# Normalisation of the second stage on ScalarE, and a re-ordered seam between two stages of a transformer block

## The reference, cut to what matters

```python
x = X                                           # 16 sequences of 512 tokens, 256 wide, fp32
x = x + attn_a(layernorm(x))                    # 16 heads of 64, softmax, exact gelu; attn_a adds its own input
x = x + ffn(layernorm(x))                       # weights quantised to -1, 0, 1; 256 -> 1024 -> relu -> 256
x = x + attn_b(layernorm(x))                    # 16 heads of 16, rotary embedding, softmax, biases
x = x + ffn(layernorm(x))                       # the same ffn again
# layernorm(x) = (x - mean) / sqrt(var + 1e-5), per token; quantise(W) = clip(round(W / (mean|W| + 1e-5)), -1, 1)
```

## Time and profile before

| | us |
|---|---|
| three runs | 3824.11, 3825.49, 3829.05 (median 3825.49) |
| the profiled execution, device time | 3828.33 |
| its span, first to last instruction | 3826.2 |
| PE busy in the span | 3658.7 (96%) |
| DVE, ACT, POOL busy | 2724.2 (71%), 2318.7 (61%), 1927.7 (50%) |
| seam, roughly | 2150 to 2300 |

### The profile page before, as it was taken

The page is one execution under the profiler, slowest core; times in us unless marked ns, Lnnn a source line. Parts: engine busy times, 40 slices in busy tenths (PEclk is TensorE's granted clock), DMA queues, the critical chain, the costliest instruction groups (busy, mean ns, idle before and its releaser), DMA issues.

```text
span 3826.2 us, 64594 instructions
## 1 busy us (share of the span) xinstructions
PE 3658.7 (96%) x23938; PEld 2458.9 (64%) x23938; DVE 2724.2 (71%) x4335; ACT 2318.7 (61%) x4501; POOL 1927.7 (50%) x1218
## 2 busy tenths in 40 slices
PE   8999999999999999999999868999999999999987
PEld 5777777777777777777777554555555555555534
DVE  6766667667666666766667757888888888887772
ACT  5666656565565656656665435666666666666654
POOL 4555555555555555555555443455555555554412
PEclk9999999999999999999999988999999999999998
DMA  2000000000000000000000022333333333333220
GB/s 78 7 12 1 12 12 12 1 12 12 1 12 12 12 1 12 12 1 12 12 4 12 24 47 51 53 58 58 58 58 62 57 59 59 56 57 57 51 46 17
DMA packets 90933, 114.15 MB, mean 30 GB/s; under 512 B 10752, under 2 KB 64384, under 8 KB 90624
## 3 DMA queue, kind: packets, MB, share of 16 engines
q1 hardware_dynamic: 90624, 110.02, 14.3%
HBM read 33.43 MB, written 25.17 MB: 15 GB/s over the span
## 4 chain that ended last, share of the span: by engine, by line
PE 82%; DVE 8%; POOL 4%; ACT 3%; issue 2%; SPq 0%; DMA 0%; DVEq 0%; POOLq 0%; ACTq 0%
PE ps_o L616 12%; PE ps_s L585 10%; PE ps_t L598 8%; PE ps_t L216 7%; PE ps_o L692 6%; PE ps_t L727 5%; PE ps_m L598 4%; PE ps_s L665 4%; PE ps_t L718 4%; PE ps_t L223 4%; PE ps_t L651 3%; PE ps_m L216 3%; DVE max_b L1090 3%; PE ps_s L679 2%; PE ps_m L718 2%
## 5 line engine op out<-in xcount | busy, mean ns | idle before, releaser
L485 POOL TENSOR_TENSOR e_a<-e_a,recip 128x1024 f32<-128x1024 f32 x512 | 969.7, 1894 | 959.4 <-DVE recip L956 959.3
L770 ACT ACTIVATE e_a<-ps_s,neg_max 128x512 f32<-128x512 f32 x1024 | 694.3, 685 | 554.2 <-DVE neg_max L949 553.8
L1090 DVE TENSOR_REDUCE max_b<-ps_s 128x2 f32<-128x1024 f32 x512 | 623.6, 1219 | 177.3 <-PE ps_s L665 175.5
L812 ACT ACTIVATE et<-ps_s 128x1024 f32<-128x1024 f32 x512 | 523.4, 1022 | 359.6 <-PE ps_s L679 359.0
L949 DVE TENSOR_REDUCE neg_max<-ps_s 128x2 f32<-128x1024 f32 x512 | 622.9, 1217 | 69.6 <-PE ps_s L585 69.6
L616 PE MATMUL ps_o<-et_a,v_a 128*64 128x256 f32 x4096 | 500.4, 386 | 7.0 <-DVE heads_a L992 1.8
L585 PE MATMUL ps_s<-raw_a 64*128 64x512 f32 x3072 | 428.3, 411 | 11.2 <-ACT e_a L770 11.1
L517 POOL TENSOR_TENSOR h_lo<-h,h_hi 128x512 fp32r<-128x512 f32 x256 | 330.2, 1304 | 178.0 <-ACT h_hi L856 178.0
L598 PE MATMUL ps_t<-ident,e_a 128*128 128x128 f32 x2660 | 395.0, 281 | 7.7 <-DVE xl L1137 5.8
L616 PEld LDWEIGHTS ps_o<-et_a,v_a 128*64 128x64 f32 x4096 | 279.6, 137 | 190.3 <-issue 76.6
L963 DVE COPY et_a<-ps_t 128x512 f32<-128x512 f32 x366 | 251.0, 688 | 204.1 <-PE ps_t L598 200.0
(11 more groups left out here) (196 smaller groups left out, 7323.5 us busy)
## 6 DMA issues: line engine op xcount, KB each, us to landing
q_stack<-roped_q SPq DMA_DIRECT2D x256, 64.0 KB
k_stack<-roped_k SPq DMA_DIRECT2D x256, 64.0 KB
x_a<-X SPq DMA_DIRECT2D x16, 512.0 KB, 3.8
X<-x_a SPq DMA_DIRECT2D x16, 512.0 KB, 2.9
x_ahead<-X SPq DMA_DIRECT2D x16, 512.0 KB, 3.8
X<-x_ahead SPq DMA_DIRECT2D x16, 512.0 KB, 4.3
q_stack<-roped_q SPq DMA_DIRECT2D x256, 32.0 KB
k_stack<-roped_k SPq DMA_DIRECT2D x256, 32.0 KB
```

The lines of the kernel that those rows point to most:

```text
L485: nc.gpsimd.tensor_tensor(e_a[:, u % 5, :, :], e_a[:, u % 5, :, :], factor, ALU.mult).then_inc(e_normed, 1)
L770: ins = nc.scalar.activation(e_a[:, u % 5, h, :], ps_s[:, 2 * (u % 2) + h, :], ACT.Exp, bias=neg_max[:, u % 5, h:h + 1], accum_out=sums[:, ...
L812: nc.scalar.activation(et[:, v % 5, :, :], ps_s[:, 2:4, :], ACT.Exp)\
L1090: nc.vector.reduce_max(max_b[:, u // 4 % 2, :, u % 4], ps_s[:, score_bank(u):score_bank(u) + 2, :], AX.X, negate=True).then_inc(max_done, 1)
```

## The change

- **Normalisation.** VectorE no longer computes (x - mean) * rstd. It computes `shift` = -mean * rstd, 128 x 4 numbers, two steps after the aggregation (`shift_of`), and ScalarE computes rstd * x + shift, with scale and shift a partition, once for each block of 128 x 256 (`normalise`, now in ScalarE's list, at the end of its step). Three norms a sequence, twelve instructions a sequence, 192 in all. Pieces four and five move from steps -103, -98 to -101, -99 (ffn0) and from -60, -58 to -59, -57 (attention); ffn1's stay at 113 and 115.
- **Seam prepared later.** W1 is quantised after slot 505 (504 before), W2 after slot 512 (506), attention b's weights are split after 514 and 515 (508, 509), the ones of `v_b` are set after 516 (514).
- **The ones of `k_stack`** are no longer set by VectorE over the whole tile; two DMAs at slot 523 put 32 KB of ones each into the four rows that need them.
- **Last heads' product later.** `LAST_POSTS` goes from slots 45, 46, 47, 48 of the last sequence to 56, 57, 58, 58 (525 to 528 becomes 536 to 538), and the last store of the first stage from slot 50 to 60. Scratch for sequence 0's roped parts and the first stack wait for it.
- **Low parts by two engines.** For sequences 0 and 1 of the first ffn, VectorE subtracts the odd blocks' low parts, GpSimd the even ones. All other sequences stay with GpSimd.

```diff
-        POST, LAST_POSTS = ((32, 32, 35, 36), (43, 44, 51, 52)), (45, 46, 47, 48)
+        POST, LAST_POSTS = ((32, 32, 35, 36), (43, 44, 51, 52)), (56, 57, 58, 58)
-        RESIDUAL, LOAD_X, SAVE_X, LAST_SAVE = 13, -22, 54, 50
+        RESIDUAL, LOAD_X, SAVE_X, LAST_SAVE = 13, -22, 54, 60
-        FIRST_A, LAST_A, LATE = -21, UNITS_ALL + 20, 4
+        FIRST_A, LAST_A, LATE = -21, UNITS_ALL + 29, 4
-        LOAD_W, LOAD_WB, LOAD_REST, SPLIT, ABS = 40, 484, 503, (508, 509), (471, 473)
-        GAMMA, QUANTISE, SCALE, CLEAR = 474, (504, 506), 514, (513, 514)
+        LOAD_W, LOAD_WB, LOAD_REST, SPLIT, ABS = 40, 484, 503, (514, 515), (471, 473)
+        GAMMA, QUANTISE, SCALE, CLEAR, KEY_ONES = 474, (505, 512), 513, 516, 523
...
-        NORM = {"ffn0": (-108, -106, -105, -103, -98), "attn": (-67, -64, -63, -60, -58), "ffn1": (103, 108, 109, 113, 115)}
+        NORM = {"ffn0": (-108, -106, -105, -101, -99), "attn": (-67, -64, -63, -59, -57), "ffn1": (103, 108, 109, 113, 115)}
...
+        def low_by_dve(n):
+            return n % 2 == 1 and n in first_ups
+        first_ups = {nth_up["ffn0", f, s] for f in range(FT) for s in range(2)}
...
+        def wait_low(engine, n):
+            if low_by_dve(n):
+                engine.wait_ge(first_low, n + 1 - lows_before[n + 1])
+            else:
+                engine.wait_ge(h_split, lows_before[n + 1])
...
                 def stack(s, pair):
+                    if s == 0 and pair == 0:
+                        wait_filled(sp, fill_of["post", 1, TB - 1, BATCH - 1])
...
+                def load_key_ones():
+                    sp.wait_ge(weights_ready, 2)
+                    sp.wait_ge(weights_split, 2)
+                    sp.wait_ge(gamma_ones, 1)
+                    for h in range(2):
+                        sp.dma_start(k_stack[64 * h + 48:64 * h + 50, :, :].bitcast(F32).rearrange("p a s -> p (a s)"),
+                                     ones[64 * h:64 * h + 64, :]).then_inc(key_ones_in, 16)
...
             @block.scalar
+                def normalise(part, s, first):
+                    act.wait_ge(shift_ready, nth_norm[part, s] + 1)
+                    if part == "ffn0" and s == 0:
+                        act.wait_ge(a_x_out, 16 * (BATCH - 1))
+                    for t in (first, first + 1):
+                        nc.scalar.activation(xn[:, t, :], x_of[part][:, t, :], ACT.Identity, scale=rstd[:, t:t + 1],
+                                             bias=shift[:, t:t + 1]).then_inc(xn_ready, 1)
...
                         if step % 2 == 0 and 0 <= step // 2 - L < UNITS_ALL:
                             exps(step // 2 - L)
+                        for piece, part, s in norm_steps.get(step, []):
+                            if piece > 2:
+                                normalise(part, s, 2 * (piece - 3))
...
                 def parts_high(i, half, s):
+                    if s == 0 and half == 0:
+                        if i == 0:
+                            act.wait_ge(parts_ready, PAIRS * BATCH)
+                        else:
+                            wait_filled(act, fill_of["post", 1, TB - 1, BATCH - 1])
...
             @block.vector
-                def set_key_ones():
-                    dve.wait_ge(a_qk_done, UNITS_ALL)
-                    nc.vector.memset(k_stack[:, :, :].bitcast(F32), 1.0).then_inc(ones_set, 1)
...
-                def normalise(part, s, first):
+                def shift_of(part, s):
                     dve.wait_ge(rstd_ready, nth_norm[part, s] + 1)
-                    if part == "ffn0" and s == 0:
-                        dve.wait_ge(a_x_out, 16 * (BATCH - 1))
-                    for t in (first, first + 1):
-                        nc.vector.tensor_scalar(xn[:, t, :], x_of[part][:, t, :], mean_var[:, t, 0:1], rstd[:, t:t + 1],
-                                                ALU.subtract, ALU.mult).then_inc(xn_ready, 1)
+                    nc.vector.scalar_tensor_tensor(shift[:, :], mean_var[:, :, 0], -1.0, rstd[:, :], ALU.mult, ALU.mult)\
+                        .then_inc(shift_ready, 1)
...
+                def first_hidden_low(part, i, s):
+                    n = nth_up[part, i, s]
+                    dve.wait_ge(hi_copied, n + 1)
+                    nc.vector.tensor_tensor(h_lo[:, i, :], h32[:, n % 4, :], h_hi[:, i, :], ALU.subtract).then_inc(first_low, 1)
```

More of the change, by code:

```diff
@@ L57, in hybrid_block_kernel @@
         minus_half = at("minus_half", 0.53125, [P, TB])
+        shift = at("shift", 1.4375, [P, TB])
         stats = at("stats", 0.5625, [P, TB, 6])
@@ L120, in hybrid_block_kernel @@
         max_b = at("max_b", 1.375, [P, 2, 2, TB])
-        recip_b = at("recip_b", 1.5, [P, S // 32])
+        recip_b = at("recip_b", 0.9375, [P, S // 32])
         token_rows = at("token_rows", 204, [P, S])
@@ L126, in hybrid_block_kernel @@
         wb_raw = [at("wb_raw0", 150.5, [P, 3 * D]), at("wb_raw1", 146, [P, 3 * D])]
-        ones = at("ones", 150, [P, P])
+        ones = at("ones", 1.5, [P, P])
         def ps(name, shape):
@@ L151, in hybrid_block_kernel @@
         ones_set = sem("ones_set")
+        key_ones_in = sem("key_ones_in")
         dve_step = sem("dve_step")
@@ L165, in hybrid_block_kernel @@
         a_xn_ready = sem("a_xn_ready")
+        shift_ready = sem("shift_ready")
         xn_ready = sem("xn_ready")
@@ L192, in hybrid_block_kernel @@
         h_split = sem("h_split")
+        first_low = sem("first_low")
         hi_copied = sem("hi_copied")
@@ L349, in hybrid_block_kernel @@
         nth_up = {(part, i, s): n for n, (_, kind, part, i, s) in enumerate(x for x in plan if x[1] == "up")}
+        def low_by_dve(n):
+            return n % 2 == 1 and n in first_ups
+        first_ups = {nth_up["ffn0", f, s] for f in range(FT) for s in range(2)}
+        lows_before = [0]
+        for n in range(2 * FT * BATCH):
+            lows_before.append(lows_before[-1] + (0 if low_by_dve(n) else 1))
+        def wait_low(engine, n):
[3 more added lines that the diff above has]
+                engine.wait_ge(h_split, lows_before[n + 1])
         x_of = {"ffn0": x_ahead, "attn": x_ahead, "ffn1": x_before}
@@ L435, in stack @@
                         sp.dma_start(k[row + 32:row + 48, pair, :], k_parts[lanes, 2, :, :]).then_inc(b_stacked[pair], 16)
+                def load_key_ones():
[5 more added lines that the diff above has]
+                                     ones[64 * h:64 * h + 64, :]).then_inc(key_ones_in, 16)
                 def max_rows(s, pair):
+                    if s == 0 and pair == 0:
+                        sp.wait_ge(key_ones_in, 2 * 16)
                     wait_emptied(sp, fill_of["max", "attn", pair, s])
@@ L462, in _ @@
                         load_rest()
+                    if slot == KEY_ONES:
+                        load_key_ones()
                     for step in (2 * (slot - SHIFT), 2 * (slot - SHIFT) + 1):
@@ L553, in _ @@
                         for kind, part, i, s, fill in steps_of.get(step - 3, []):
-                            if kind == "up":
+                            if kind == "up" and not low_by_dve(nth_up[part, i, s]):
                                 hidden_low(part, i, s)
@@ L722, in product @@
                             if i == 0:
-                                pe.wait_ge(h_split, nth_up[part, f, s] + 1)
+                                wait_low(pe, nth_up[part, f, s])
                             if part == "ffn0" and s == 0 and f == 0 and i == 0:
@@ L849, in hidden_high @@
                     wait_emptied(act, fill)
-                    if n == 0:
-                        act.wait_ge(weights_ready, 2)
                     if i == 0:
@@ L1008, in split_wb @@
                         for m in range(KT):
-                            nc.vector.tensor_tensor(wb_lo[:, m, :], wb_raw[m][:, :], wb_hi[:, m, :], ALU.subtract)
+                            ins = nc.vector.tensor_tensor(wb_lo[:, m, :], wb_raw[m][:, :], wb_hi[:, m, :], ALU.subtract)
+                        ins.then_inc(weights_split, 1)
                 def absolute_sum(i):
@@ L1174, in _ @@
                             empty_low(*todo)
+                        for kind, part, i, s, fill in steps_of.get(step - 3, []):
+                            if kind == "up" and low_by_dve(nth_up[part, i, s]):
+                                first_hidden_low(part, i, s)
                         if step % 2 == 0 and 0 <= step // 2 < UNITS_ALL:
@@ L1181, in _ @@
                                 aggregate(part, s)
-                            else:
-                                normalise(part, s, 2 * (piece - 3))
+                        for piece, part, s in norm_steps.get(step - 2, []):
+                            if piece == 2:
+                                shift_of(part, s)
                         for s in range(BATCH):
@@ L1204, in _ @@
                         scale_biases()
-                    if slot == CLEAR[0]:
-                        set_key_ones()
-                    if slot == CLEAR[1]:
```

(1 more changed line is left out.)

6 lines of the change are left out of this document (1 added, 5 removed).

## The result

The changed kernel took 3869.1 us in the median of four runs (3865.8 to 3882.1), before 3824.8: the ratio is 1.0115 with a 95% interval of 1.010 to 1.013. Predicted were 3839, in a range of 3830 to 3848, and slower. The direction was right; the size was not, and the time lies above the range.

The account below looks back on a forecast made before the run. PE was taken as nearly full in steady rounds, with long holes at the seam, and ScalarE as fuller at the critical places. Seam -20.4, rest +37 - 3 + 1: +14 us, from the median 3839.6; forecast 3839, range 3830 to 3848.

Parts of the forecast that it names:

- ScalarE's price: One 128x256 normalising instruction on ScalarE: some 0.56 us long, 0.46 us of the queue each, 0.93 a pair.
- ffn1's window: Steady part, steps 113 and 115 (49, 51): two pairs on ScalarE make PE wait 1.4 us, in 13 sequences.
- Attention's window: Steady part, steps -59 and -57 (5, 7): both pairs precede an exponential PE awaits; 1.45 us, in 13 sequences.
- What VectorE gives back: VectorE's freed normalisations hold GpSimd up less on the chain of rotary products: 0.2 us a round, 3 us (0 to 8).
- Tail: End of the first stage: with weight preparation moved later, the last values start at 2183.5 instead of 2195.9, -12.4 us.
- The moved work: Just after the first stage: VectorE's share of low parts queues behind the moved weight splitting, +1 us.
- Middle: Seam, before attention's transposes of sequence 0: with the last heads' product later, the 8.69 us hole ends earlier, -4.5 us.
- the prediction's own sign: Check on the seam: `up` products that started at 2258.32 come near 2242.5; after 2248, the seam step is wrong.
- Low parts: Sequence 1 in the seam: with two engines the last low part ends at about 2271.5 instead of 2273.4, -1.5 us.
- First units: Second stage's first units, bound by VectorE: its normalisation leaves their chain and a shift comes, -3 us (-1 to -4).
- End: The last norm is on the path: four ScalarE pieces of 0.46 us plus the shift against VectorE alone, +1 us.
- the round doesn't have the slack that I read: Rival, steady rounds: all engines shift together, two pairs cost their full 3.7 us a round, 3851; last two rivals 0.10 together.

Follow-up runs that it names:

- queue_two: The kernel before with the exponentials of steps 6 and 8 both done twice, all normalisation on VectorE; 3863.2 us, ratio 1.0091 to before.
- posts_back: The changed kernel with all normalisation back on VectorE and the last heads' product in its old slots 45 to 48; 3817.0 us, ratio 0.9972 to before.
- low_pool: The changed kernel with all normalisation back on VectorE and all low parts on GpSimd again; 3818.9 us, ratio 0.9971 to before.
- seam_ffn1: The changed kernel with ffn1's normalisation alone on ScalarE, the other norms back on VectorE; 3837.1 us, ratio 1.0021 to before.
- attn_late: The changed kernel with ffn1's norm on VectorE, attention's ScalarE pieces and GpSimd's bias nine steps later, attention's transposes two; 3885.8 us, ratio 1.0147 to before.

## Why the prediction was right and wrong

- *ScalarE's price: right.* 0.56 us predicted, 0.593 to 0.600 measured, a pair 0.98 of the queue for 0.93. The 213 ns and the 85 ns in that sum stand in no row of before, whose rows give 198 and 62. By the formula in the Trainium skill, "ScalarE: Activation LUTs", What ACT_TABLE_LOAD costs, the estimate was 585 ns and 0.49 in the queue; the trace (0.49 from one to the next) agrees better with it than with my sum.
- *ffn1's window: right.* 1.4 us predicted, 1.55 by the stretch of 31.06. The new holes are 0.37 and 0.62 where 0.5 and 0.8 were named.
- *Attention's window: the queue right, the step that failed is the one behind it.* "all of 1.86 counts but the hole of 0.40 ...: 1.45 us". Without a clock fall it is 1.6, and the round 96.60 us, where 96.4 stood. But I priced the longer hole as waiting alone and read from the earlier trace rows a clock of 1.00 as given. The hole of 1.76 is followed by a lower clock in 8 or 9 rounds of 12, for 0.9 to 2.3 us each: some 13.5 us over the twelve in either profile of the changed kernel. queue_two shows that ScalarE's queue does it without the instruction. A row for this price stood in the trace of before: behind its hole of 1.25 the stretch of ffn0's norm is 33.40 us where it is 31.53 without a fall.
- *What VectorE gives back: right place, too small.* 0.2 us a round predicted, on the chain of rotary products; ffn0's stretch lost 0.3 to 0.6 in the mean, by the profile of before that one takes, some 5 us. The hole of 1.25 at the end of that chain is gone from the changed kernel, and with it the falls behind it (stretches of 31.9 to 33.4).
- *`shift_of`: wrong price, no effect.* 0.2 us assumed; 0.99 in the mean. It is in 44 of 48 cases done before ScalarE asks.
- *Seam: too large.* Tail 10.4 for 12.4 predicted. The moved work: the +1 was 3.5, since post additions, not only low parts, queue behind wb_hi and wb_lo, as the hole of 2.50 shows. Middle: 0 for 4.5, by posts_back. The heads were not all that held PE there: without them it waits for attention's xn of sequence 0. By the prediction's own sign (`up` products of sequence 1 after 2248) the step is wrong: they start at 2251.38. Low parts: the lead grows by 2.7 from there to attention's rstd of sequence 1 (2276.0, before 2285.6), of which low_pool puts 1.5 down to the second engine, as predicted. First units 4.3 for 3. Together -10.4 + 3.5 - 2.7 - 4.3 = -13.9 instead of -20.4; it is the 2411.6 of ffn1's rstd of sequence 0, which stands at 2425.3 to 2426.2 in four profiles of before.
- *End: +1 predicted.* From attention's last rstd, 3615, to the end the changed kernel takes 252.4 and 250.2 us, the kernel before 243.5 to 247.5: some 6 more, of which 2.7 to 4 are a thirteenth attention window with its fall; the rest lies within the clock's spread there.

Sum: -14 at the seam, 13 x 1.55 + 12 x 1.6 = +39 for the windows, -5 relief, +13.5 clock, +6 end: +39.5. The two profiles of the changed kernel have spans 40.5 and 41.4 above the mean of before's four (3826.2); the medians say +44 and +39. The prediction's +14 (14.6 by its terms) lacked the 13.5 of the clock, 6 of the seam, 5 at the end and 2 in the windows, and had the relief 2 too small.

Of the rivals, "the round doesn't have the slack that I read" came nearest by its number (3851) and is wrong by its mechanism: seam_ffn1 leaves the other stretches as they were.

## What to carry to other kernels

An engine's mean load says little of the place where work is moved to; here the fuller engine had room at every place, and the emptier one had none at two of three. Where a hole of PE grows, price two things: the wait, and what the slower clock behind it would cost, from a row that shows it; look for such a row in every stretch, not in one round. And when an instruction is moved, ask what it dates: here the place of one xn set when the next x was loaded.

## What was not expected of the hardware

- A single wait of TensorE of 1.76 to 1.90 us, in a stretch in which it is otherwise busy, was followed by 3.4 to 6.8 us at the 1.2 GHz level in 7 to 10 of 12 rounds; one of 2.86 in all 12, for up to 10 us; waits of 0.46 and 0.75 us some 3 us apart never. Elsewhere one of 1.25 was followed by it in 2 to 7 of 12 rounds, and of attn_late's twelve waits for xl three of 2.87 to 3.13 were not.
- A 128x4 instruction with two SBUF inputs on VectorE took 141 ns at the least, 968 in the median and 1252 at the most. The six of 141 to 163 ns have no GpSimd instruction beside them; the 42 longer ones (647 and up) lie beside GpSimd's of 1.3 to 1.5 us with two SBUF inputs. The Trainium skill, "SBUF — State Buffer", Who interferes with whom, calls the port pair that the two engines share an exclusive lock; the trace agrees, the small one waits for up to 1.2 us of a large one.
